# Joins moved to SyncE, first results kept in the join buffers, and the first expert tile inside the last attention group

## The reference

```python
xn = _layernorm(x)
x = x + linear_attention0(xn) + moe0(xn)      # 16 heads; 8 experts of 176 (silu gate), 2 per token, plus a shared one
xn = _layernorm(x)
x = x + attention1(xn) + moe1(xn)
# attention1: q, k = elu(.), energy = (q k^T) * causal mask, out = energy v, rms-normed, gated by silu(u), times Wo
# moe1: logits -> softmax -> top 2 of 8 experts; gelu(x w1 + b1) w2 + b2, 512 hidden, weighted by the two gates
```

## Time and profile before

| | us |
|---|---|
| median of 3 runs | 913.72 (912.93 to 915.83) |
| the profiled execution | 911.97 |
| its span in the trace | 910.3 |
| PE busy | 834.7 (92%) |
| VectorE busy | 700.4 (77%) |
| ScalarE busy | 576.1 (63%) |
| GpSimd busy | 621.6 (68%) |
| attention of layer 1 | about 412 to 640 |
| experts of layer 1, first to last second product | 654.0 to 898 |

### The profile page before, as it was taken

The page is one execution under the profiler, slowest core; times in us unless marked ns, Lnnn a source line. Parts: engine busy times, 40 slices in busy tenths (PEclk is TensorE's granted clock), DMA queues, the critical chain, the costliest instruction groups (busy, mean ns, idle before and its releaser), DMA issues.

```text
span 910.3 us, 22670 instructions
## 1 busy us (share of the span) xinstructions
PE 834.7 (92%) x7975; PEld 744.4 (82%) x7975; DVE 700.4 (77%) x1809; ACT 576.1 (63%) x1183; POOL 621.6 (68%) x598
## 2 busy tenths in 40 slices
PE   3789999999899999998898989898899899999996
PEld 3678878989799999986665666666899899999996
DVE  7787777886576998897899998898664555667776
ACT  5766465444477667769887777573666566666661
POOL 4156676777304788777888888887777777666663
PEclk9999999999999999999999999999999999999999
DMA  9799997115649999962111111115664665588985
GB/s 268 234 373 357 361 353 258 50 50 161 244 143 270 311 314 279 277 212 75 40 43 37 39 40 44 37 44 187 220 186 151 199 193 189 165 246 273 285 276 174
DMA packets 131136, 174.30 MB, mean 191 GB/s; under 512 B 15825, under 2 KB 85969, under 8 KB 130769
## 3 DMA queue, kind: packets, MB, share of 16 engines
q1 hardware_dynamic: 96864, 124.43, 42.8%
q0 software_dynamic: 16640, 34.37, 11.5%
q10 hardware_dynamic: 17520, 14.06, 5.1%
HBM read 93.96 MB, written 80.97 MB: 192 GB/s over the span
## 4 chain that ended last, share of the span: by engine, by line
PE 59%; DVE 25%; issue 5%; ACT 5%; POOL 4%; DMA 2%; SPq 0%; DVEq 0%; ACTq 0%; POOLq 0%
PE pair L923 14%; PE pair L892 6%; PE pair L861 5%; PE pair L862 5%; PE pair L863 5%; PE pair L695 3%; PE pair L782 3%; DVE a_en L1622 3%; POOL sent L2064 2%; DVE X L1555 2%; PE pair L702 2%; DVE stats_t L1184 2%; PE pair L704 2%; PE pair L703 2%; DVE X L1642 1%
## 5 line engine op out<-in xcount | busy, mean ns | idle before, releaser
L2064 POOL DMA_INDIRECT sent<-a_rows,slot x224 | 220.9, 986 | 77.8 <-issue 57.4
L2075 POOL DMA_INDIRECT ex_joined<-outs,slot x128 | 136.4, 1066 | 82.5 <-DMA outs<-ex_tile_out 45.6
L2166 POOL DMA_INDIRECT back<-ex_tile_out,address x136 | 150.1, 1104 | 59.2 <-issue 31.4
L861 PE MATMUL pair<-ex_x_hi,ex_w_hi 128*128 128x256 f32 x497 | 146.9, 296 | 0.0
L862 PE MATMUL pair<-ex_x_lo,ex_w_hi 128*128 128x256 f32 x497 | 140.7, 283 | 0.0
L863 PE MATMUL pair<-ex_x_hi,ex_w_lo 128*128 128x256 f32 x497 | 140.5, 283 | 0.0
L923 PE MATMUL pair<-ex_down_all,ex_hid 128*128 x1136 | 133.3, 276 | 1.1 <-ACT ex_hid L1888 0.8
L923 PEld LDWEIGHTS pair<-ex_down_all,ex_hid 128*128 128x128 f32 x1136 | 129.7, 192 | 2.7 <-issue 2.7
L1762 ACT ACTIVATE ex_w_hi<-ex_stage 128x768 fp32r<-128x768 f32 (+1 forms) x72 | 67.5, 937 | 69.6 <-DMA ex_stage<-in_experts 69.6
L1888 ACT ACTIVATE ex_hid<-pair,ex_stage 128x256 f32<-128x256 f32 x284 | 107.7, 494 | 4.5 <-PE pair L863 2.2
L863 PEld LDWEIGHTS pair<-ex_x_hi,ex_w_lo 128*128 128x128 f32 x497 | 95.1, 191 | 0.0
(11 more groups left out here) (253 smaller groups left out, 2021.3 us busy)
## 6 DMA issues: line engine op xcount, KB each, us to landing
outs<-v_heads SPq DMA_DIRECT2D x8, 4352.0 KB, 37.3
ex_stage<-in_experts SPq DMA_DIRECT2D x72, 322.0 KB
ex_stage<-in_experts SPq DMA_DIRECT2D x72, 320.0 KB, 5.1
ex_tile_in<-sent SPq DMA_DIRECT2D x72, 128.0 KB
outs<-ex_tile_out SPq DMA_DIRECT2D x71, 128.0 KB
ex_joined<-back ACTq DMA_DIRECT2D x15, 512.0 KB, 5.9
ex_tile_in<-sent SPq DMA_DIRECT2D x54, 132.0 KB
X<-in_x SPq DMA_DIRECT2D x16, 256.0 KB, 5.3
```

The source lines that it names most:

```text
L861: pe.matmul(o[:, of_half], wh, x_hi[i % 2][:, of_half], start=True, stop=False)
L2064: pool.indirect_dma_start(out=sent[layer], out_offset=bass.IndirectOffsetOnAxis(ap=slot_i[layer][k][:, s, j:j + 1], axis=0), in_=rows[laye ...
L2075: pool.indirect_dma_start(out=joined[g % NJOIN][:, j, k, :], out_offset=None, in_=outs, in_offset=bass.IndirectOffsetOnAxis(ap=slot_i[0][k ...
L2166: pool.indirect_dma_start(out=back, out_offset=bass.IndirectOffsetOnAxis(ap=address[i % NSIDE][:, s // HALF, s % HALF:s % HALF + 1], axis= ...
```

## The change

- **Homes of results.** The results of tiles 0 to 5 of layer 1 are not written to `tile_out` but to the halves of the three `joined` buffers, and weighing waits for a returned buffer only from tile 10 on. Addresses get a place for each tile, gates two buffers (`NGATE`).
- **Returns.** GpSimd first issues all 32 sends of the last super group (`SENDS_LAST`), then returns tiles 6, 7, 8, 0, 9, 10, 1, 11, 2, 12, 3, 13, 4, 14, 5, 15 and on in order (`BACK_ORDER`).
- **First tiles.** `EARLY` is 7, so 12 tiles start before all is sent.
- **Joins.** SyncE issues them, in its own turns 28 to 35 (`JOINS`), behind the weights of the turn, and the last four after its loop. VectorE adds in its turns 26 to 34 (`ADDS`), ScalarE stores a turn later.
- **Sends and gathers in attention** are spread anew over the steps, seven or eight a step, and from step 16 on without waits for PE.
- **Masks of the last two groups.** ScalarE copies one pair also there, and VectorE masks the copy (`mask_copied`).
- **End of attention.** Steps 18 and 19 are written out: energies of the last group, sums, transposes of tiles 0 and 1, and the four products of tile 0 stand among the last sums and outputs; the third and fourth use banks 6 and 7. The third product of tile 1 waits for the last addition of attention (`x_new`).

```diff
+SENDS_LAST = (3, 0, 32)
+EARLY = 7
+LATE_STEP = 16
+NEXTRA = 2 * NJOIN
+JOINS = {28: (0,), 29: (1, 2), 30: (3,), 31: (4, 5), 32: (6,), 33: (7, 8), 34: (9,), 35: (10, 11)}
+ADDS = {26: (0,), 27: (1, 2), 28: (3,), 29: (4, 5), 30: (6,), 31: (7, 8), 32: (9,), 33: (10, 11), 34: (12,)}
+STORES = {n + 1: groups for n, groups in ADDS.items() if n + 1 < NTILES}
+FIRST_BACK = {8: 0, 10: 1, 11: 2, 12: 3, 13: 4, 14: 5}
+BACK_ORDER = [m for n in range(NEXTRA, LAST_BACK + 1) for m in ((n, FIRST_BACK[n]) if n in FIRST_BACK else (n,))]
...
                 if n >= NSTAGE[1]:
                     sp.wait_ge(out_ready, i - NSTAGE[1] + 1)
                 load_weights(1, n, experts)
-                if n == 0:
+                if n == 1:
                     sp.dma_start(flat(down_all[:]), t["down1"]).then_inc(weight1_dma, 16)
-            results_back(sp, NTILES + LAST_BACK)
-            load_results(sp, 2 * NG - 1)
+                for g in JOINS.get(n, ()):
+                    results_back(sp, NTILES + last_tile(1, g))
+                    load_results(sp, NG + g)
+            for g in range(sum(map(len, JOINS.values())), NG):
+                results_back(sp, NTILES + min(last_tile(1, g), LAST_BACK))
+                load_results(sp, NG + g)
...
             for n in range(NTILES + 1):
                 if n >= 2:
                     weigh1(n - 2)
-                if n in LAST_ADD and n <= LAST_BACK + 1:
-                    collect1(LAST_ADD[n])
-                if n + 1 < NTILES:
+                for g in ADDS.get(n, ()):
+                    collect1(g)
+                if 1 <= n < NTILES - 1:
                     split_weights(1, n + 1)
                     split_rows(1, n + 1, 4)
...
+            e, y = NG - 1, NG - 2
+            energies(e, 0)
+            energies(e, 1)
...
+            by_columns(2, 0, ones[:, 0:NARROW], sq1[:]).then_inc(sums_done, 1)
+            from_state(e)
+            gather(e, 0)
...
+            sums_to_rows(2, 0, 1).then_inc(ss_done, 1)
+            rows_to_columns(1, 0, 0)
+            gather(e, 1)
+            pe.wait_ge(tot_here, y + 1)
+            output1(y)
...
+            by_columns(5, 0, ones[:, 0:NARROW], sq1[:]).then_inc(sums_done, 1)
+            up1(0, 0)
...
+            sums_to_rows(5, 0, 1).then_inc(ss_done, 1)
+            up1(0, 1)
+            rows_to_columns(1, 1, 4)
+            up1(0, 2)
...
+            output1(NG - 1)
+            up1(0, 3)
...
+            def mask_copied(e, s):
+                i = 2 * e + s
+                dve.wait_ge(en_copied, i + 1)
+                dve.tensor_tensor(blocks(en1[1][i % 2][:]), blocks(en1[1][i % 2][:]),
+                                  const("causal").unsqueeze(1).to_broadcast([P, 8, P]), ALU.mult).then_inc(en_masked, 1)
```

More of the change, by code:

```diff
@@ L177, in logits_bank, with bank_of_up1 @@
 def logits_bank(layer, step):
-    return 6 if layer == 0 or step == 1 else 2
+    return 6 if layer == 0 or step == 1 else 5 if step == NG + LEAD + 1 else 2
+def bank_of_up1(n, c):
+    return c + 4 if n == 0 and c >= 2 else c
 def has_sums(layer, step):
@@ L1081, in tensor_program @@
             pe.wait_ge(consts1_made, 1)
-            for step in range(LEAD, STEPS1):
+            for step in range(LEAD, NG + LEAD):
                 g, e, y = step - LEAD, step - LEAD - 1, step - LEAD - 2
@@ L1975, in totals @@
                 total = rms[:, y % 2, 0, :] if with_root(y) is None else bases[:, y % 2, 0:GT]
[L1976 to L1978 removed]
+                act.activation(total, blocks(bank[logits_bank(1, y + LEAD + 2)][:, 0:P], NARROW)[:, :, 0], ACT.Copy).then_inc(tot_here, 1)
+            for step in range(LEAD, NG + LEAD):
                 g, e, y = step - LEAD, step - LEAD - 1, step - LEAD - 2
@@ L1985, in scalar_program @@
                     squares(y)
-                if step == NG + LEAD + 1:
-                    split_weights(1, 0)
-                if old and not masked_by_dve(e):
+                if old:
                     copy_energies(e, 0)
@@ L2226, in pool_program @@
                         roots_and_deviation(y, n)
-                transfer(7)
-            for n in range(NTILES):
-                if n in SENDS_LAST:
-                    s, first, end = SENDS_LAST[n]
-                    for i, jk in enumerate(range(first, end)):
-                        if n == 0:
-                            behind_tile1(i // NC1, i % NC1)
-                        else:
-                            behind_tile1(n + 1 + (i + 3) // NC1, (i + 3) % NC1)
-                        send(1, s, jk)
-                if n <= LAST_BACK:
-                    give_back(n)
+                for i in range(7, len(gathers) + len(sends)):
+                    transfer(i)
+            s, first, end = SENDS_LAST
+            for jk in range(first, end):
+                send(1, s, jk)
+            for n in BACK_ORDER:
+                give_back(n)
         sync_program()
```

173 lines of the change are left out of this document (102 added, 71 removed), and 6 rows, old and new, of the table SENDS.

## The result

The changed kernel takes 961.1 us (median of four runs, 959.88 to 967.46) against 914.8 us for the kernel before beside it (912.93 to 917.65): a ratio of 1.052, 95% interval 1.046 to 1.057. The forecast was 957.5, counted up from 913.7; of the 3.6 us between it and the median, 1.1 is the higher median of the kernel before. The profiled execution took 960.32 us with a span of 958.7, 48.4 more than the span of before.

A forecast was written before the change was run, and what follows sets the result against it. PE was taken as the bound, with VectorE handing it work. Terms +48.7 - 5.2 + 1 - 0.5 + 1.4 - 1.4 = +44.0 us on 913.7 gave 957.7, taken as 957.5; range 936 to 975.

The forecast's parts named there:

- The mechanism that carried the forecast: Turns 26 to 33: SyncE can issue a join only after the weighing just before its addition, so VectorE waits.
- the joins: Expert stage, joins moved to SyncE's queue and later: cost +48.7 us, between +32.7 and +65.
- attention: Attention of layer 1: GpSimd has fewer transfers per step but nobody waits for it there, so no term.
- The rings of turns: Turns 26 to 33: VectorE's wait sets each turn, 12.1 us with one join, 14.0 with two.
- The wait W: VectorE, from the end of weighing until the join has landed: 6.6 us, bounds 4.9 and 8.2.
- The stall: PE's 3.78 us wait at tile 10 goes: -5.2 us, range -5.2 to -3.
- The root: End of attention: GpSimd's last root comes at about 649 behind eight sends, leaving -0.5 us, range -6 to +1.
- rival 4: End of attention: the root is in time, 5.5 us less, 952; no chance of its own given.
- The returns: Expert stage: GpSimd's queue returns tile 15 late, so weighing of tile 19 waits: +1 us, range 0 to 3.
- The tail: After the last tile: group 12 is added in turn 34 and the last join doesn't wait for it: -1.4 us.
- the clock: Join turns: PE's idleness brings the low clock back, hidden seven times, showing once after the last: +1.4 us.

The follow-up runs named there:

- e1: Changed kernel with each join one turn of SyncE earlier: 1080.8 us on the slower chip, where the kernel before took 1014.5.
- e10: Kernel of e9 with each group's addition one turn of VectorE later: 903.4 us, ratio 0.986 to the kernel before.
- e2: Kernel before with only the changed kernel's joins, additions and stores: 1075.3 us on the slower chip, ratio 1.060 to the kernel before there.
- e3: Changed kernel with a turn's joins issued ahead of that turn's weights: 1096.8 us on the slower chip (kernel before 1014.5).
- e7: Changed kernel with EARLY back at 6, so SyncE stops again before tile 10 until all sends have landed: 961.2 us.
- e5: Changed kernel with the former tables of sends and gathers in attention, and 24 sends left for the end: 959.8 us.
- e8: Changed kernel with joins one SyncE turn earlier and two instead of eight sends between the last two roots: 911.6 us, ratio 0.994 to the kernel before.
- c1: Changed kernel unchanged, run again on another chip: 961.7 us, ratio 1.048 to the kernel before.
- e9: Kernel of e8 with the first six tiles' returns spread, behind tiles 8, 10, 13, 15, 17 and 19: 913.0 us.
- e4: Changed kernel with two instead of eight sends between the roots of groups 14 and 15: 1121.2 us on the slower chip (kernel before 1014.5).

## Why the prediction was right, and where it wasn't

The mechanism that carried the forecast is the one that the runs show. That the sum came as near as 4.4 us (+48.4 against +44.0) is in part luck: the joins cost 6.6 us more than forecast, and attention, which had no term, gave back 4.7.

**The joins: right mechanism, undersized by 6.6 us.** The rings of turns are where I placed them, from the addition of group 0 on, one group in four of them and two in four. The wait W was forecast at 6.6 us; in the turns with one group it was 6.98, 7.28, 7.08 and 6.95. A turn with one group took 12.7 us from one set of transposes to the next (12.1 forecast), one with two groups 15.2 (14.0): in them the first addition waited 6.7 to 8.3 us and the second followed 1.7 to 2.3 us later. Between the transposes of tile 28 and those of tile 35 lie three of the first kind and four of the second: 0.6 x 3 + 1.2 x 4 = 6.6 us over the forecast. The term that was too small is the wait. Of the 0.5 us that it was short with one group, 0.2 are the issue: the join left 1.39 us after the weighing in seven of the eight turns, not 1.2, as SyncE's own waits took 0.3 and not 0.1. The rest is the time from issue to use: I took 5.4 us from the one join on SyncE's queue, which had no weights ahead of it; behind weights it was 5.6 to 5.9, and where a second join left with the first, 5.0 to 6.9. e1 and e10 show that the cost goes with the distance in turns between issue and use, e2 that the joins alone make all of the loss, and e3 that it depends on what is issued ahead of the join, which no row of before shows.

By the cost model of the Trainium skill (DMA: Bandwidth & Descriptors, Anatomy of one DMA), fitted there to transfers that GpSimd issues, such a join would take 3.2 us, as an estimate. The shortest of the sixteen in the changed kernel took 3.8, so for these joins the fit was a lower end, and the trace decides against it.

**The stall: right size, half a reason.** -4.7 against -5.2. Of the two reasons given, that no return stands between the sends and that tile 12 is the first to need them all, e7 shows the first to be too little by itself. The second without the first was not run.

**Attention: the step that failed.** I wrote that GpSimd has fewer transfers per step, but that nobody waits for it there, and set 0. That stretch was 4.7 us shorter, and e5 gives 3.8 of them back with the table alone. In the window from 500 to 575 PE is busy 68.42 us in before and e5 (68.43), and 69.47 in the changed kernel. Which of GpSimd's results PE had waited for isn't shown by any one row: the chain goes over masks and powers to VectorE and from there to PE, in parts of under 1 us each.

**The root: right mechanism, and a second one.** I forecast the last root at 649 and the stretch half a microsecond shorter; the root was done at 644.9, since attention was earlier, and the stretch was 1.2 us longer. VectorE's wait for the root and PE's for the addition were there as described. Taking six sends away from between the roots shortened it by 7.5 us (e8); rival 4 had priced that at 5.5.

**The returns: right size for the wrong quantity.** I counted GpSimd's queue, expected tile 19 to wait and priced it at +1; +1.6 was measured. But I took it for an accident of one tile. It is nearly a ceiling: with the starts taken off, e8 weighs tile 0 7.5 us earlier than c1 and tile 24 only 1.2 us earlier, e9 6.0 and 0.6. A gain ahead of it counts only as far as GpSimd's 84 returns allow; the root's is the one for which this was run. The term came out near all the same, since in the changed kernel PE and GpSimd arrive there almost together: PE loses 1.7 us, between the transposes of tiles 22 and 23 (785.93 to 794.47).

**The tail and the clock.** -1.6 against -1.4. The granted clock fell to 0.84 in the stretch of the joins, as I had it from the low clock after the stall, and its cost was covered by VectorE's turns; I had counted 1.4 us for its last turn, and no row separates them from the 56.7.

The range was 936 to 975. Its ends came from landings of 3.7 and 7.0 us; the measured ones (median 5.9, 3.8 to 8.5) lie inside the first and beyond the second for single transfers.

## What to carry to other kernels

When a transfer moves to another queue, read two places: what the issuing engine waits for just ahead of it, and what the user of the data does just ahead of using it. If both are the same instruction, the whole landing is on the path in every turn, however early the table's numbers look. One turn more on SyncE's side showed no cost here and was worth 48 us (c1 to e8) to 51 us (e4 to e1); the last 7 to 9 us came back with a turn more on VectorE's side as well, which was not run alone. And before gains of several stages are added up, look for an engine that has a fixed list of work between the first stage and the last: its list ends when it ends, and most of what the others gained ahead of it was handed back there.

## What the runs showed of the hardware

**A landing depends on what is issued ahead of it.** A join of 512 KB on SyncE's queue took 3.8 to 8.5 us in the changed kernel, median 5.9 (median 6.4 in e10, 8.3 in e2), and from issue to use 4.2 us ahead of the turn's weights (e3) and 5.7 behind them (e4).

**GpSimd's indirect transfers keep a steady pace.** 0.97 us and a pause of 0.30, for sends and returns alike, some of them 1.3 to 2.0; without a longer wait, the 84 returns of e9 took 115.7 us from the first issue to the last. GpSimd is busy 64% of the span of the changed kernel by its page and yet sets the pace there for some 100 us: the pauses don't count as busy, and the share is a mean over the stages.

**One chip was 11% slower for the kernel before, and more for the new one.** e4 took 1121.2 us there, 17% over the 961.1 of the changed kernel, from which it differs by six sends. The difference is not spread evenly. In e1 there, behind the attention, PE got its instructions one by one while GpSimd issued sends without a pause; nothing that the profile shows ended PE's waits (the window, with the columns as above, two of PE's instructions, and VectorE's wait):

```profile
740.00:790.00 50.00, 18.33 (x67) 12.93 (x67) 3.08 (x9) 5.08 (x12) 33.83 (x35) 0.57 0.15 51
...
774.11 0.37 PE L903 MATMUL pair<-ex_x_hi,ex_w_lo 128*128 128x256 f32 x1 [2.43 <-issue]
776.21 0.37 PE L901 MATMUL pair<-ex_x_hi,ex_w_hi 128*128 128x256 f32 x1 [1.73 <-issue]
...
789.67 0.69 DVE L1595 TENSOR_TENSOR ex_joined<-pair,ex_b2o 128x512 f32<-128x512 f32 x1 [46.74 <-remote]
```

The transfer engines were busy 0.15 then, so it wasn't their load. On that chip e1, e3 and e4, which have the new order of sends, weighed tile 24 at 995.5, 985.3 and 983.2; e2, with the former order, at 933.6. So the new order loses some 50 us there that it doesn't lose on the other chips. That the late instructions come of the unbroken series of indirect transfers is not shown, only that both stand side by side; no run was made to separate them, and why this chip differs stays open. Whoever compares kernels has to run them on one chip, and should know that a change can be worth different things on two.
